# A transformer block with two fp4 feed-forwards: another order of the feed-forward's steps, ScalarE makes all magic numbers, attention's last turns without silu, some of their copies on VectorE

## The reference

```python
def fp4_quant_dequant(x):            # blocks of 16 along the last dim
    scale = max(max(|xb|) / 6, 1e-12)
    idx = searchsorted(_MID, |xb / scale|)
    return _GRID[idx] * sign(xb) * scale      # grid 0, .5, 1, 1.5, 2, 3, 4, 6
def fp4_linear(x, w): return quant(x) @ quant(w).T
def ffn(x):                          # 128 -> 352 -> 128
    h = silu(fp4_linear(x, w_gate)) * fp4_linear(x, w_up)
    return fp4_linear(h, w_down)
def attn(x):                         # 16 heads of 8, causal, 256 tokens
    softmax(Q K^T / sqrt(8)) V Wo + bo
x = x + 0.5 * ffn(layernorm(x))
x = x + attn(layernorm(x))
x = x + 0.5 * ffn(layernorm(x))
```

## Time and profile before

| | us |
|---|---|
| median of 3 runs | 508.67 (508.06 to 512.35) |
| profiled execution | 511.76 |
| its span in the trace | 509.8 |
| TensorE busy (PE) | 416.4 |
| VectorE busy (DVE) | 419.7 |
| ScalarE busy (ACT) | 310.8 |
| GpSimd busy (POOL) | 258.9 |

### The profile page before, as it was taken

How to read it: one execution, slowest core, us unless ns; L and a number is a source line. 1 busy time by engine, 2 the same in 40 slices (tenths; PEclk the granted TensorE clock), 3 DMA queues, 4 the chain that set the end, 5 groups by cost and what they waited for, 6 DMA issues and landing times.

```text
span 509.8 us, 12742 instructions
## 1 busy us (share of the span) xinstructions
PE 416.4 (82%) x3625; PEld 305.8 (60%) x3625; DVE 419.7 (82%) x1154; ACT 310.8 (61%) x841; POOL 258.9 (51%) x467
## 2 busy tenths in 40 slices
...
GB/s 214 196 1 2 0 1 0 0 1 93 149 145 146 70 127 130 133 130 112 134 135 136 136 136 137 122 21 5 2 0 2 12 11 21 21 21 10 21 23 31
DMA packets 30543, 35.52 MB, mean 70 GB/s; under 512 B 1699, under 2 KB 27299, under 8 KB 28195
## 3 DMA queue, kind: packets, MB, share of 16 engines
...
...
## 4 chain that ended last, share of the span: by engine, by line
PE 42%; DVE 15%; issue 11%; ACT 4%; POOL 1%; DVEq 1%; POOLq 0%; ACTq 0%
PE bank L1215 8%; PE bank L1187 7%; PE bank L1242 6%; PE bank L1184 5%; PE bank L1246 3%; PE bank L1164 2%; DVE nm L985 2%; ACT hq_magic L616 2%; PE bank L1272 2%; DVE f_h L956 1%; DVE hq_grid L834 1%; PE bank L1171 1%; PE bank L1079 1%; PE bank L1257 1%; PE bank L1078 1%
## 5 line engine op out<-in xcount | busy, mean ns | idle before, releaser
L734 ACT ACTIVATE probs<-bank 128x512 f32<-128x512 f32 x192 | 112.6, 602 | 67.0 <-PE bank L1215 64.1
L985 DVE TENSOR_REDUCE nm<-bank 128x2 f32<-128x512 f32 (+1 forms) x192 | 126.7, 682 | 15.0 <-PE bank L1187 13.9
L581 POOL TENSOR_SCALAR_AFFINE_SELECT probs<-probs 128x256 f32<-128x256 f32 (+1 forms) x192 | 91.6, 485 | 93.0 <-ACT probs L734 91.0
L1215 PE MATMUL bank<-q_stack,k_stack 75*128 75x256 bf16 (+1 forms) x512 | 76.3, 252 | 4.0 <-ACT probs L734 2.5
L1187 PE MATMUL bank<-k_stack,q_stack 72*128 72x256 bf16 (+1 forms) x512 | 74.7, 247 | 0.0
L515 POOL TENSOR_TENSOR xq_out<-xq_grid,xq_scale 128x256 f32<-128x256 bf16 x32 | 25.3, 790 | 89.5 <-DVE xq_grid L834 89.5
L1098 PE MATMUL bank<-ident,hq_out 128*128 128x128 f32 (+1 forms) x192 | 33.7, 286 | 42.4 <-ACT f_hT L677 40.4
L1184 PE MATMUL bank<-causal,ident_bf 128*128 128x256 bf16 (+1 forms) x192 | 60.2, 314 | 3.3 <-DVE nm L985 2.8
L1098 PEld LDWEIGHTS bank<-ident,hq_out 128*128 128x128 f32 (+1 forms) x192 | 22.3, 141 | 64.5 <-ACT f_hT L677 36.5
L616 ACT ACTIVATE hq_magic<-hq_exps 128x704 bf16<-128x704 bf16 x28 | 22.1, 790 | 62.7 <-DVE hq_exps L820 62.7
L1107 PE MATMUL bank<-wdT,f_hT 128*128 128x128 f32 (+1 forms) x384 | 57.1, 286 | 1.6 <-ACT f_hT L677 1.6
...
## 6 DMA issues: line engine op xcount, KB each, us to landing
...
q_stack<-nmT SPq DMA_DIRECT2D x16, 24.0 KB
```

Of the source, the lines that this page charges most:

```text
L581: nc.gpsimd.affine_select(out=v, in_=v, compare_op=ALU.is_ge, fill=0.0, base=0, pattern=[[0, heads], [1, P]], channel_multiplier=-1).then_ ...
L734: nc.scalar.activation(probs[:, c, :], ps[:, :], ACT.Exp, scale=SCALE).then_inc(done, 1)
L985: nc.vector.tensor_reduce(nm[:, j, h0:h0 + n], ps[:, :].rearrange("p (h k) -> p h k", h=n), AX_X, ALU.max, negate=True).then_inc(done, 1)
L1215: last = nc.tensor.matmul(ps[:, w * n:w * n + w], k_stack[0:SROWS, s, HG * g + h, k0:k0 + P], q_stack[0:SROWS, s, HG * g + h, q0:T], start ...
```

## The change

The order and the lags of the feed-forward's steps are new: lnV moves a turn later (lag 1), dn1 a turn earlier (the turn of dn0), and a turn now goes xT, gates 0, hT0, lnV, gates 1, hT1, dn0, hq, xq, xr, h0, h1, hr, dn1, lnN, lnS. VectorE therefore makes the products h0 and h1 of the next batch between the exponents and the sums of the batch in hand. The products no longer wait for the whole quantisation of the batch before, only for its fourth instruction (HNORMED). ScalarE makes the magic number of x as well as that of h, except where VectorE makes it itself in the first and last batches. x goes ahead of h in each pair, and sum and grid of one follow each other. In the lists where phases meet, the second feed-forward's gates of batch 0 move from attention's turn 20 to turn 21, behind the last exponential of batch 15, and those of batch 1 from turn 21 to turn 22. In these turns VectorE makes some copies that ScalarE made (VECTOR_COPIES: of batches 14 and 15, 14, 13 and 14, and batch 0 of the feed-forward). The loop of the attention is the same.

The diff, without the hunks in which ScalarE returns early from oc0, oc1 and yTc, in which round_weights puts x first, and the second half of VectorE's y_copy:

```diff
 QSTEPS = 8
 QEXPS = 6
+HNORMED = 4
...
 FFN_LAG = {step: lag for lag, steps in enumerate((
-    "lnS lnV",
-    "lnN",
+    "lnS",
+    "lnV lnN",
     "xq xr",
     "xT gu0 h0 gu1 h1",
     "hq hr",
-    "hT0 hT1 dn0",
-    "dn1",
+    "hT0 hT1 dn0 dn1",
 )) for step in steps.split()}
-FFN_ORDER = "xT lnS dn1 hq xq gu0 xr hr h0 hT0 gu1 lnN hT1 lnV dn0 h1".split()
+FFN_ORDER = "xT gu0 hT0 lnV gu1 hT1 dn0 hq xq xr h0 h1 hr dn1 lnN lnS".split()
 FFN2_ORDER = [step for step in FFN_ORDER if step not in ("lnS", "lnV")]
 FFN2_LAG = {step: max(0, FFN_LAG[step] - 1) for step in FFN2_ORDER}
 FFN_UNROLL = 2
@@ -90,42 +90,39 @@
 NM_TURNS = ATT_UNROLL - 1
 
 
-FFN1_END = 13
+FFN1_END = 12
 FFN_TURN = " ".join(f"f.{step}" for step in FFN_ORDER)
 WARM = """
-third f.xT lnN f.lnS f.dn1 xT xTc f.hq stack lnS lnA lnE f.xq f.gu0 qk f.xr f.hr c1 f.h0 f.hT0 f.gu1 split f.lnN
-f.hT1 f.lnV f.dn0 f.h1 bias c2 v
+third f.xT lnN f.gu0 xT xTc f.hT0 f.lnV stack f.gu1 qk f.hT1 c1 f.dn0 f.hq lnS f.xq f.xr f.h0 lnA split f.h1 lnE f.hr f.dn1
+c2 f.lnN f.lnS bias v
 """
 FIRST_SCORES = """
-third f.xT lnN f.dn1 xT xTc f.hT0 f.gu0 f.hT1 f.gu1 f.dn0 qk f.hq stack c1 f.hr f.h0 f.h1 split S0 S1 S2 c2 S3 lnS S4 lnA S5
+third f.xT lnN f.gu0 xT xTc f.hT0 f.gu1 qk f.hT1 stack c1 f.dn0 f.hq f.h0 f.h1 split f.hr f.dn1 S0 S1 S2 c2 S3 lnS S4 lnA S5
 lnE S6 bias S7 v S8 S9 S10 S11
 """
 FIRST_PROBS = """
-nmS third f.dn1 lnN S0 f.hT0 S1 nm f.hT1 xT xTc S2 f.hq f.dn0 stack qk S3 ST0 c1 S4 f.hr ST1 S5 split ST2 S6 lnS ST3 S7 lnA
+nmS third lnN S0 f.hT0 S1 nm f.hT1 xT xTc S2 f.hq f.dn0 f.dn1 stack qk S3 ST0 c1 S4 f.hr ST1 S5 split ST2 S6 lnS ST3 S7 lnA
 c2 S8 lnE bias S9 v ST4 S10 S11
 """
-FIRST_VALUES = "nmS f.dn1 ST5 S0 f.hT0 third  ST6 lnN S1 f.hT1 nm  ST7 S2 f.dn0 stack  ST8 S3"
-REST_VALUES = """
-f.dn1 xT xTc bias  ST9 S4  ST10 S5 AV0 AV1 lnS  ST11 oc0 lnA S6  ST0 lnE S7 qk
-ST1 c1 S8  ST2 split S9 AV2 AV3  ST3 c2 oc1 S10 v  ST4 S11
+FIRST_VALUES = """
+nmS ST5 S0 f.hT0 third  ST6 lnN S1 f.hT1 nm  ST7 S2 f.dn0 f.dn1 stack  ST8 S3 xT xTc bias  ST9 S4  ST10 S5 AV0 AV1 lnS
+ST11 oc0 lnA S6  ST0 lnE S7 qk  ST1 c1 S8  ST2 split S9 AV2 AV3  ST3 c2 oc1 S10 v  ST4 S11
 """
 FULL = " ".join(ATT_ORDER)
-FFN_TO_ATT = [(13, None, FFN_TURN), (14, 0, WARM), (15, 1, WARM), (16, 2, WARM), (17, 3, WARM), (18, 4, FIRST_SCORES),
-              (19, 5, FIRST_PROBS), (20, 6, FIRST_VALUES), (21, 6, REST_VALUES), (None, 7, FULL)]
-LAST_PROBS = "nmS ST5 f.xq oT0  ST6 n0  ST7 nm  ST8 f.xr oT1 n1 AV0 AV1  ST9 oc0 yT"
-FIRST_GATES = """
-f.xq f.xT f.lnN  ST10 yTc wo  ST11 f.xr wa AV2 AV3  ST0 sS  ST1 oc1 sA  ST2 sE  ST3  ST4 f.gu0 f.gu1 f.h0 f.h1
+FFN_TO_ATT = [(12, None, FFN_TURN), (13, None, FFN_TURN), (14, 0, WARM), (15, 1, WARM), (16, 2, WARM), (17, 3, WARM),
+              (18, 4, FIRST_SCORES), (19, 5, FIRST_PROBS), (20, 6, FIRST_VALUES), (None, 7, FULL)]
+LAST_PROBS = """
+nmS ST5 oT0 n0  ST6 f.xq nm  ST7 oT1  ST8 n1 AV0 AV1  ST9  ST10  ST11 yT f.xr oc0 yTc  ST0  ST1  ST2  ST3 AV2 AV3  ST4
 """
+LAST_RESIDUAL = "wo f.xq oc1 wa sS sA sE"
 LAST_VALUES = """
-f.xT  ST5 oT0 n0  ST6 oT1 n1  ST7 yT f.lnN  ST8 AV0 AV1 yTc  ST9 oc0 wo  ST10  ST11 f.hq f.xq f.xr f.hr wa AV2 AV3 f.gu0 oc1 f.gu1
-f.h0 sS f.h1 sA sE
+ST5 f.xT  ST6  ST7 oT0  ST8 AV0 AV1 n0  ST9  ST10 f.xr  ST11 f.gu0 oT1 f.gu1 n1 oc0 yT yTc AV2 AV3 f.h0 wo f.h1 oc1 wa f.lnN
 """
-LAST_OUTPUT = """
-f.xT oT0 f.hq n0 f.xq f.gu0 oT1 f.xr f.hr n1 f.h0 f.hT0 f.gu1 yT yTc f.lnN f.hT1 wo f.dn0 f.h1 wa sS sA sE
-"""
+LAST_OUTPUT = "f.xT f.gu0 oT0 f.gu1 f.hq f.xq f.xr n0 f.h0 oT1 n1 f.h1 f.hr yT yTc f.lnN wo wa sS sA sE"
 ATT_TO_FFN = [(0, 16, FULL.replace("ST4", "f.lnN ST4")), (1, 17, FULL.replace("ST4", "f.lnN ST4")), (None, 18, FULL), (None, 19, FULL),
-              (1, 20, LAST_PROBS), (2, 20, FIRST_GATES), (3, 21, LAST_VALUES), (4, 22, LAST_OUTPUT),
-              (5, None, " ".join(f"f.{step}" for step in FFN2_ORDER))]
+              (1, 20, LAST_PROBS), (2, 20, LAST_RESIDUAL), (2, 21, LAST_VALUES), (None, 21, "sS sA sE"), (3, 22, LAST_OUTPUT),
+              (4, None, " ".join(f"f.{step}" for step in FFN2_ORDER))]
+VECTOR_COPIES = {"oc0": (14, 15), "oc1": (14,), "yTc": (13, 14), "f.xT": (0,)}
...
+def copied_by_vector(step, b):
+
+    return isinstance(b, int) and b in VECTOR_COPIES[step]
...
     ffn2.loop(eng)
-    ffn2.peeled(range(ffn2.end, ffn2.stop - 2))
-    ffn2.step("dn1", ffn2.stop - 2, ffn2.stop - 2)
+    ffn2.peeled(range(ffn2.end, ffn2.stop - 1))
     for name in LAST_ORDER:
         if name in last:
...
@@ -624,6 +625,7 @@
 
                 def h_magic(b, s, it):
                     if not alone(b):
+                        magic(xquant, b + base + ALONE)
                         magic(hquant, b + base)
 
                 def x_sums(b, s, it):
@@ -653,6 +655,8 @@
                     nc.scalar.copy(x_all[:, b, :, :].rearrange("p j c -> p (j c)"), ps.dn[:, 0:NT * C]).then_inc(x_ready, 1)
 
                 def x_copy(b, s, it):
+                    if base and copied_by_vector("f.xT", b):
+                        return
                     act.wait_ge(f_xT_filled, b + base + 1)
                     if base or not first(b, 2):
...
@@ -820,19 +828,17 @@
                     nc.vector.tensor_scalar(q.exps[:, :].bitcast(I16), q.odd[:, :].bitcast(I16), EXP_BITS, None,
                                             ALU.bitwise_and).then_inc(q.step, 1)
 
-            def round_fp4(*jobs, magic_here=False):
+            def round_fp4(*jobs, magic_here=()):
 
                 for q, s, n in jobs:
-                    if q is xquant or magic_here:
+                    if q in magic_here:
                         dve.wait_ge(q.step, QSTEPS * n + QEXPS)
                         nc.vector.tensor_scalar(q.magic[:, :], q.exps[:, :], MAGIC_MUL, MAGIC_ADD, ALU.mult, ALU.add).then_inc(q.magic_ready, 1)
                 for q, s, n in jobs:
                     dve.wait_ge(q.magic_ready, n + 1)
                     nc.vector.tensor_tensor(q.sum[:, :], q.odd[:, :], q.magic[:, :], ALU.add).then_inc(q.step, 1)
-                for q, s, n in jobs:
                     dve.wait_ge(q.step, QSTEPS * n + QEXPS + 1)
                     nc.vector.tensor_tensor(q.grid[:, s, :], q.sum[:, :], q.magic[:, :], ALU.subtract).then_inc(q.step, 1)
-
 
...
@@ -937,13 +943,13 @@
                     elif alone(b):
                         quantise(h_job(b, s))
                     else:
-                        quantise(h_job(b, s), x_job(b + ahead, (s + ahead) % FFN_UNROLL))
+                        quantise(x_job(b + ahead, (s + ahead) % FFN_UNROLL), h_job(b, s))
 
                 def round_both(b, s, it):
                     if halved(base, b):
                         return
                     if alone(b):
-                        round_fp4((hquant, s, b + base), magic_here=True)
+                        round_fp4((hquant, s, b + base), magic_here=(hquant,))
                     else:
                         round_fp4((xquant, (s + ahead) % FFN_UNROLL, b + base + ahead), (hquant, s, b + base))
 
@@ -952,11 +958,17 @@
                         n = b + base
                         dve.wait_ge(silu_ready[j], n + 1)
                         if base or not first(b, 1):
-                            dve.wait_ge(hquant.step, QSTEPS * n)
+                            dve.wait_ge(hquant.step, QSTEPS * (n - 1) + HNORMED)
                         nc.vector.tensor_tensor(f_h[:, j, :], f_silu[:, j, :], ps.up[j][:, 0:I], ALU.mult).then_inc(h_ready[j], 1)
                     return f
 
-                steps = {"xq": quantise_x, "xr": round_x, "hq": quantise_both, "hr": round_both}
+                def x_copy(b, s, it):
+                    if base and copied_by_vector("f.xT", b):
+                        dve.wait_ge(f_xT_filled, b + base + 1)
+                        dve.wait_ge(gu_filled[NT - 1], b + base - 1)
+                        nc.vector.tensor_copy(f_xT[:, s, :], ps.xT[:, 0:T]).then_inc(f_xT_read, 1)
+
+                steps = {"xq": quantise_x, "xr": round_x, "hq": quantise_both, "hr": round_both, "xT": x_copy}
                 steps.update({f"h{j}": gate_up(j) for j in range(NT)})
                 return ffn_pipeline(base, steps)
...
@@ -1017,6 +1029,20 @@
                 xb = x_all[:, b, :, :].rearrange("p j c -> p (j c)")
                 nc.vector.tensor_tensor(xb, ps[:, 0:NT * C], xb, ALU.add).then_inc(done, 1)
 
+            def o_copy(pair):
+                def f(b, s, it):
+                    if copied_by_vector(f"oc{pair}", b):
+                        dve.wait_ge(filled["AV"], GROUPS * b + 2 * pair + 2)
+                        dve.wait_ge(filled["oT"], NT * (b - OT_TURNS + 1))
+                        nc.vector.tensor_copy(oT[:, s % OT_TURNS, pair, :], att_ps[AV_BANK][:, 0:T]).then_inc(taken["AV"], 1)
+                return f
+
+            def y_copy(b, s, it):
+                if copied_by_vector("yTc", b):
```

(13 more changed lines are left out.)

8 lines of the change are left out of this document (5 added, 3 removed).

## The result

The changed kernel takes 512.95 us (median of 20 runs, 510.3 to 518.03) against 508.63 for the kernel before (20 runs on the same chip, 506.76 to 513.41). The ratio is 1.0098, 95% interval 1.007 to 1.0125: slower by 1%, where 1.5% faster was forecast. The profiled execution took 513.8 us, span 512.0, against 511.76 and 509.8. Executions of one kernel differ by some microseconds, and the longer ones show a lower mean granted clock (the changed kernel 0.953 to 0.956 around 512 to 514 us and 0.943 around 517; the kernel before, in the runs beside e1 to e4, about 0.972 around 507.3 and 0.955 around 512.5), so the kernel before, with 0.959 in its profiled execution, was profiled in one of its longer ones.

The account below looks back on a forecast made before the run. It took VectorE to bound both feed-forwards and no engine attention's end. Terms +2.5 + 1.0 - 0.8 - 8 - 2.6 = -7.9 us turn the median 508.67 into 500.8 us (chance 0.52), range 487 to 510.

Parts of the forecast that it names:

- Attention's end, -8: Stretch between attention loop and second feed-forward's steady turns: 8 us saved, bounds -12 and -2, including two fewer table loads.
- the sign: At attention's end, VectorE would idle under 3 us in one piece if the forecast held.
- Start, +2.5: Before turn 7: slow gates delay sums, down copy and lnN; turn 6 begins near 45.1, +2.5 us (0 to +4).
- Ring and turn, +1.0 for turns 7 to 13: First feed-forward's loop-like turns go from 7.15 to about 7.3 us each: +1.0 us, bounds -4 and +2.
- the ring: Feed-forward loop: dn1, down copy, lnN, sums, next xT copy and gates, without VectorE, set the turn at 7.3 us.
- rival (c): Feed-forward: TensorE's wait of 2.1 us halves its clock in some turns; 522 us at one in three; chance 0.08.
- Turns 14 to 19, -0.8: Turns with attention's first steps: ring plus attention products about 8.8 us in 15 and 16; -0.8 us, -3 to +2.
- Pairing sum and grid of each job exposes about 0.04 us of latency twice: VectorE's feed-forward turn: each job's grid following its sum costs only this, leaving VectorE alone 6.5 to 6.6 us.
- rival (a): VectorE runs free in both feed-forwards at 6.55 us a turn: -19.8 us, 488.9 by the median; chance 0.13.
- Second feed-forward, -2.6: Its 12 turns go from 7.16 to 6.95 us by a longer two-turn ring: -2.6 us, bounds -7 and 0.
- Magic numbers on ScalarE: Feed-forward: x's number takes ScalarE about 0.41 us, covered by VectorE's two products, 0.95; xsum waits about 0.1.

Follow-up runs that it names:

- e1: The changed kernel with dn1 issued last, behind lnN and the sums, in the feed-forward's turn and turns 14 to 17: 504.17 us, ratio 0.9927.
- e4: The changed kernel with three filler matmuls, never read, behind dn1 in each turn of its two loops: 511.66 us, ratio 1.0042.
- e2: The kernel before with only attention's last-turn lists, VectorE's copies there and the earlier release of f_h: 498.62 us, ratio 0.9835.
- e12: e1 with three filler matmuls per turn in the first feed-forward's loop and turns 14 to 17: 504.6 us, ratio 0.9918.
- e9: e7 with both sums ahead of both grids again in the first feed-forward: 499.03 us, ratio 0.98.
- e3: The changed kernel with h ahead of x in VectorE's paired quantisation: 515.92 us, ratio 1.0167.
- e7: First feed-forward and turns 14 to 20 as before, attention's end and second feed-forward as e1, each grid behind its sum: 503.47 us, ratio 0.9925.
- e6: e1 with x's magic number made by VectorE instead of ScalarE: 514.64 us, ratio 1.0141.
- e8: The kernel before with only x's magic number moved to ScalarE: 520.19 us, ratio 1.0191, from few runs.

## Why the prediction was wrong

**Attention's end, -8: right.** -9.27 in the profile; e2, without the new order of the feed-forward, has -7.85. Two table loads are gone, as foretold. VectorE's longest wait there is 3.67 us (before 385.60), where under 3 was named as the sign. Some of the 9.27 may be luck of the execution: with the same lists the stretch took 36.5 us in e1 at a clock of 0.91, and 40.0 in e4 at 0.83.

**Start, +2.5: right.** +1.85; turn 6 began at 44.41, forecast 45.1.

**Ring and turn, +1.0 for turns 7 to 13: the ring is right, the term is not.** 7.29 and 7.32 against 7.3; at seven turns the ring costs 7 x (7.32 - 7.15) = 1.2. The other 3.0 are two falls of the clock. The step that failed is that the term took the clock over as 1.00 from the earlier trace rows and left its fall to rival (c): the mechanism was named with its gap of 2.1 us (2.17 in the trace), but given a chance of 0.08, because the earlier trace rows shows 1.00 beside a gap of 1.69. The size was off as well, 1.5 us for a fall in place of 3: a fall slowed only a part of the turn's work (the last two windows of the first fence), and the turn grew by 1.5. The Trainium skill (TensorE: Matmul & The Clock Gate, Part 1), cited there for idle stretches that bring the clock to its lower level, was the right warning; e4, where the falls go with the gap filled, bears it out.

**Turns 14 to 19, -0.8: the step that failed most.** It was +4.87 in turns 14 to 17 and about +1.0 behind them. The forecast added attention's products to the ring (8.8 us each in turns 15 and 16) and gave VectorE's extra statistics 7.5 and 8.5 in turns 14 and 17. Found were 7.41, 9.39, 10.13 and 12.07. So turn 14 came out, and the miss grows to the last. Turn 17, with VectorE's wait for attention's c1 in it, and in the second fence the same turn of e1:

```profile
132.80:144.87 12.07, 10.34 (x44) 7.36 (x43) 10.01 (x26) 6.10 (x16) 5.40 (x8) 0.73 0.53 149
141.94 0.69 DVE L988 TENSOR_TENSOR qk_rest<-bank,qk_parts 128x512 f32<-128x512 f32 x1 [1.99 <-ACT qk_parts L710]
```

```profile
128.10:138.06 9.96, 7.64 (x44) 5.54 (x42) 9.89 (x25) 6.22 (x16) 5.39 (x8) 1.00 0.56 149
```

At a clock of 0.73 (it is at half from about 132.5 to 139.3) the turn is 2.1 us longer than at 1.00: that part is the clock again. The rest, about 3 us over the old order, stands at whole clock too (36.99 in e12 against 33.81 in e9). The forecast names no hold-up of VectorE's rows there, but beside GpSimd's hq_out and third parts they are held up, and VectorE is busy 8.93 us in turn 15 and 10.06 of the 10.13 in turn 16; the ring's 8.8 isn't what those turns show. That these hold-ups set the turns is read from busy times; e3 didn't test it, since it moved them and removed none. The cause of this part stays open to that extent. The pairing of sum and grid costs 1.7 there in the old order (e7 less e9, with one stretch at half clock in e7).

**"Pairing sum and grid of each job exposes about 0.04 us of latency twice": wrong.** It costs 0.26 to 0.33 us a turn (e7 against e2 and e9), since GpSimd's rescale of x now starts ahead of h's grid and holds it up. In the changed kernel's first feed-forward the ring hides it. It is most of what makes VectorE need 6.9 us a turn and not 6.5 to 6.6, so rival (a) could not have come true even with the ring gone (e1).

**Second feed-forward, -2.6:** -0.67. Eleven of the turns average 6.94 (forecast 6.95); the twelfth holds a stretch at half clock and took 8.94, and that is the difference.

**Magic numbers on ScalarE: right, with their condition.** Inside the new order they gain 0.14 to 0.20 us a turn (e6), alone they lose 0.47 a turn (e8).

**The sum.** Of the 10.1 us between forecast (-7.9) and span (+2.2), 6.7 lie in the turns from 14 to attention's end, 3.2 in turns 7 to 13, 1.9 in the second feed-forward and 0.2 in the end; start and attention's end give back 1.9. By the medians the change is +4.3; the kernel before stood 3.1 above its own in the profiled execution, the changed one 0.85. The kernel before was profiled in one of its longer executions, as its granted clock says (0.959), so the stages' sum of +2.2 understates the change by about 2 us, and in which stage isn't known.

e2 (498.62) and e9 (499.03) beat both kernels; by their intervals neither is faster than the other.
